# First attention: who empties the head accumulators, and where their two parts are summed

## What is computed

```python
q_r = jnp.einsum('bshq,hqr->bhsr', q_big, W_qr)
k_r = jnp.einsum('bld,hdr->bhlr', kv_r, W_kr)
scores = jnp.einsum('bhsr,bhlr->bhsl', q_r, k_r)
attn = jax.nn.softmax(scores, axis=-1)
ctx_c = jnp.einsum('bhsl,bld->bhsd', attn, kv_r)
ctx_lat = jnp.einsum('bhsd,hkd->bhsk', ctx_c, w_kc_kv)
...
return ctx @ Wo.T
```

## Time and profile before

| | us |
|---|---|
| median of three executions | 1758.19 (1757.7 to 1759.88) |
| the profiled execution, its own time | 1745.59 |
| its span in the trace | 1743.8 |
| TensorE matmul busy | 1652.9 (95%) |
| VectorE busy | 1367.3 (78%) |
| ScalarE busy | 980.1 (56%) |
| GpSimd busy | 924.9 (53%) |

### The profile page before, as it was taken

How to read it: one execution, slowest core, us unless ns; L and a number is a source line. 1 busy time by engine, 2 the same in 40 slices (tenths; PEclk the granted TensorE clock), 3 DMA queues, 4 the chain that set the end, 5 groups by cost and what they waited for, 6 DMA issues and landing times. The chain is left out here.

```text
span 1743.8 us, 48870 instructions
## 1 busy us (share of the span) xinstructions
PE 1652.9 (95%) x16173; PEld 1309.8 (75%) x16173; DVE 1367.3 (78%) x3288; ACT 980.1 (56%) x1903; POOL 924.9 (53%) x620
## 2 busy tenths in 40 slices
PE   5889999999999999999999999999997799997998
PEld 4678888888888888888888888887875445556876
DVE  6888888888988898988889888987874278884223
ACT  5776666666666666666666666665331266662211
POOL 5347777777777777777777777775002022211321
PEclk8699999999999999999999999999998999997999
DMA  9721121121121121122112116113810000005244
GB/s 255 242 67 38 51 72 44 48 74 42 42 81 41 42 70 53 43 61 62 45 48 74 42 47 144 46 50 110 183 25 23 16 13 16 15 7 176 95 150 142
DMA packets 166253, 126.16 MB, mean 72 GB/s; under 512 B 73914, under 2 KB 153448, under 8 KB 165824
## 3 DMA queue, kind: packets, MB, share of 16 engines
q1 hardware_dynamic: 164672, 121.60, 24.7%
q0 software_dynamic: 1536, 3.99, 0.6%
HBM read 82.11 MB, written 24.41 MB: 61 GB/s over the span
## 5 line engine op out<-in xcount | busy, mean ns | idle before, releaser
L1178 POOL TENSOR_TENSOR c_rest<-c_prob 128x1024 f16<-128x1024 f32 (+1 forms) x513 | 799.4, 1575 | 329.6 <-ACT c_prob L962 309.9
L962 ACT ACTIVATE c_prob<-c_psS,ln,c_exp_scale 128x1024 f32<-128x1024 f32 (+1 forms) x514 | 536.9, 1045 | 258.1 <-PE c_psS L797 253.0
L1062 DVE TENSOR_REDUCE c_mxp<-c_psM 128x1 f32<-128x400 f32 (+1 forms) x1040 | 587.0, 571 | 95.0 <-PE c_psM L781 84.5
L797 PE MATMUL c_psS<-c_q,c_kk 128*128 128x256 f16 (+1 forms) x3350 | 512.7, 272 | 0.2 <-issue 0.2
L816 PE MATMUL c_psV<-c_vb,c_prob 128*128 128x129 f16 (+1 forms) x3328 | 396.6, 222 | 0.0
L797 PEld LDWEIGHTS c_psS<-c_q,c_kk 128*128 128x128 f16 (+1 forms) x3350 | 321.9, 99 | 85.7 <-issue 0.4
L819 PE MATMUL c_psV<-c_vb,c_rest 128*128 128x65 f16 (+1 forms) x3328 | 374.1, 193 | 0.0
L781 PE MATMUL c_psM<-c_kkm,c_q 128*128 128x400 f16 (+1 forms) x1040 | 346.1, 333 | 4.6 <-DVE c_mxp L1062 3.0
L816 PEld LDWEIGHTS c_psV<-c_vb,c_prob 128*128 128x128 bf16 (+1 forms) x3328 | 303.8, 97 | 20.5
L819 PEld LDWEIGHTS c_psV<-c_vb,c_rest 128*128 128x128 f16 (+1 forms) x3328 | 301.4, 99 | 21.4
L743 PE MATMUL c_psQ<-c_xb,c_w2s 128*128 128x256 f16 x1188 | 171.2, 276 | 10.5 <-PEq L163 4.1
(11 more groups left out here) (292 smaller groups left out, 2167.6 us busy)
## 6 DMA issues: line engine op xcount, KB each, us to landing
c_w2s<-w_scr SPq DMA_DIRECT2D x66, 256.0 KB, 2.6
c_ms<-m_scr SPq DMA_DIRECT2D x67, 192.0 KB, 2.3
c_w2s<-w_scr SPq DMA_DIRECT2D x66, 128.0 KB, 2.0
acc_scr<-c_acc SPq DMA_DIRECT2D x128, 64.0 KB, 1.6
kv<-acc_scr SPq DMA_DIRECT2D x16, 512.0 KB, 6.5
m_w<-in_L_ffn_W SPq DMA_DIRECT2D x16, 352.0 KB, 4.1
c_vb<-V SPq DMA_DIRECT2D x27, 129.0 KB, 2.0
c_kk<-KK SPq DMA_DIRECT2D x27, 128.0 KB, 2.0
```

The lines of the kernel that those rows point to most:

```text
L797: mm = pe.matmul(psS[g % 2][0:r, i * S:(i + 1) * S], src[:, (lo + i) * P:(lo + i) * P + r], mov[slot][:, :], start=(one == 0 and i % 2 == ...
L962: nc.scalar.activation(prob[g][0:r, 0:w], psS[g % 2][0:r, 0:w], ACT.Exp, bias=keep["ln1024"][0:r, :], scale=exp_scale[slot][0:r, :]).then_ ...
L1062: nc.vector.tensor_reduce(mxp[:, st, c:c + 1], psM[:, st, 0:CHUNKS[c][1]], AX.X, ALU.max).then_inc(mx_done, 1)
L1178: nc.gpsimd.tensor_tensor(rest[g][0:r, 0:w], prob[g][0:r, 0:w], high[0:r, 0:w], ALU.subtract).then_inc(rest_done, 1)
```

## The change

The VectorE drain is taken apart.

- ScalarE copies all 258 columns of `c_psV` into `c_acc`, which grows to 128 x 2 x 129 (two buffers as before). The copy stands at the end of each head's turn, behind `exp(n+1, 1)` and, at odd u, ahead of the `q_other` that opens the next head. It signals `pv_drained`, now once per head.
- GpSimd adds the low to the high sums in place and copies the two denominators into `rec` (`total`), for head n-1 in the turn of head n, between `rest_of(n, 3)` and `rest_of(n+1, 0)`. In turn 0 it does so on a buffer of zeros; `total(N)` follows the loop. So head n has row n+1 of `acc_scr` and of `rec`.
- SyncE's store waits for `total` and takes 64 of each 129 columns.
- The reciprocals are made in two instructions instead of 128: VectorE inverts the 32 denominators of the first batch behind the loop, and the other 224 at the head of the next block.

```diff
         queue.dma_start(keep["acc"][b % 2][:, s],
-                        t["acc_scr"][b * H0:(b + 1) * H0, :, s, :].rearrange("h p d -> p h d")
+                        t["acc_scr"][b * H0 + 1:(b + 1) * H0 + 1, :, s, :].rearrange("h p d -> p h d")
                         ).then_inc(keep["in_acc"][b % 2], 16)
...
     compute.tensor_tensor(rows, rows,
-                          keep["rec"][:, b * H0:(b + 1) * H0, s:s + 1].broadcast_to([P, H0, DC]),
+                          keep["rec"][:, b * H0 + 1:(b + 1) * H0 + 1, s:s + 1].broadcast_to([P, H0, DC]),
                           ALU.mult).then_inc(keep["cs_ready"], 1)
...
     W = 2 * DC + 1
-    acc = [sb(f"c_acc{i}", [P, ST, DC]) for i in range(2)]
+    acc = [sb(f"c_acc{i}", [P, ST, W]) for i in range(2)]
     psS = [ctx.enter_context(nc.psum_tensor(f"c_psS{i}", [P, 1024], F32)) for i in range(2)]
...
     zeroed, filled = sem("c_zeroed"), sem("kk2_filled")
+    acc_zeroed, summed, inverted = sem("acc_zeroed"), sem("summed"), sem("inverted")
     v_ones, v_high, v_low = sem("v_ones"), sem("v_high"), sem("v_low")
...
             sp.sem_inc(sent[0], 16)
-            sp.sem_inc(sent[1], 16)
 
...
                     refill_values(sp, last, 2)
-                sp.wait_ge(pv_drained, 2 * n + 2)
-                sp.dma_start(t["acc_scr"][n], acc[u % 2][:]).then_inc(sent[u % 2], 16)
+                sp.wait_ge(summed, 2 * n + 2)
+                sp.dma_start(t["acc_scr"][n], acc[(u + 1) % 2][:, :, DC:2 * DC]).then_inc(sent[(u + 1) % 2], 16)
                 if last is not None and u == 1:
...
                 if last is not None and u == 3:
+                    sp.wait_ge(pv_done, 4 * n + 8)
                     refill_values(sp, last, 3)
...
             for u in range(2):
-                sp.wait_ge(sent[u], 16 + 16 * (H0 // 2))
+                sp.wait_ge(sent[u], 16 + 16 * H0)
             sp.dma_start(keep["wvo"], keep["wvo_made"][:]).then_inc(keep["in_wvo"], 16)
...
             batch_steps(B - 1, 0)
+            sp.wait_ge(summed, 2 * N + 2)
+            sp.dma_start(t["acc_scr"][N], acc[1][:, :, DC:2 * DC]).then_inc(sent[1], 16)
             for u in range(2):
...
                 if g == 0:
-                    if not isinstance(n, int) or n > 0:
-                        pe.wait_ge(pv_drained, 2 * n)
+                    pe.wait_ge(pv_drained, n + 1)
                 if t0 == 0:
...
             act.sem_inc(exp_done, 2)
+            act.sem_inc(pv_drained, 1)
             for b in range(4):
...
                     exp(n + 1, 1, (u + 1) % AHEAD)
+                    act.wait_ge(pv_done, 4 * n + 8)
+                    act.wait_ge(sent[u % 2], 16 * (2 * j + u // 2) + 16)
+                    nc.scalar.activation(acc[u % 2][:].rearrange("p s w -> p (s w)"), psV[:, 0:ST * W],
+                                         ACT.Copy).then_inc(pv_drained, 1)
 
...
                                                op1=ALU.subtract).then_inc(v_low, 1)
-
-            def drain(n, u, j):
-                dve.wait_ge(pv_done, 4 * n + 8)
-                dve.wait_ge(sent[u % 2], 16 * (2 * j + u // 2) + 16)
-                both = psV[:, 0:ST * W].rearrange("p (s w) -> p s w", s=ST)
-                nc.vector.tensor_reduce(acc[u % 2][:],
-                                        both[:, :, 0:2 * DC].rearrange("p s (t d) -> p s d t", t=2),
-                                        AX.X, ALU.add).then_inc(pv_drained, 1)
-                nc.vector.reciprocal(keep["rec"][:, bass.ds(n, 1), :].rearrange("p o s -> p (o s)"),
-                                     both[:, :, 2 * DC]).then_inc(pv_drained, 1)
 
...
             v_rest(7)
-            dve.wait_ge(v_low, B)
             scale_of(0, 0)
...
                         q_low(p, u - 1)
-                        drain(n, u, j)
                     reduce_max(n + 2, 6)
-                    if u % 2 == 0:
-                        drain(n, u, j)
                     scale_of(n + 2, (u + 2) % AHEAD)
                     reduce_max(n + 2, 7)
+            dve.wait_ge(summed, 2 * H0 + 2)
+            first = keep["rec"][:, 1:H0 + 1, :]
+            nc.vector.reciprocal(first, first).then_inc(inverted, 1)
+            dve.wait_ge(inverted, 1)
             dve.wait_ge(keep["in_acc"][0], 32)
...
 
+            def total(n, i):
+
+                pool.wait_ge(pv_drained, n + 1)
+                nc.gpsimd.tensor_tensor(acc[i][:, :, DC:2 * DC], acc[i][:, :, DC:2 * DC], acc[i][:, :, 0:DC],
+                                        ALU.add).then_inc(summed, 1)
+                nc.gpsimd.tensor_copy(keep["rec"][:, bass.ds(n, 1), :].rearrange("p o s -> p (o s)"),
+                                      acc[i][:, :, 2 * DC]).then_inc(summed, 1)
+
             nc.gpsimd.memset(kk2[0:2 * SHIFT_ROWS, :], SHIFT_ONE).then_inc(filled, 1)
...
                 nc.gpsimd.memset(V[:, b, :, 2 * DC:2 * DC + 1], 1.0).then_inc(v_ones, 1)
+            nc.gpsimd.memset(acc[1][:], 0.0).then_inc(acc_zeroed, 1)
             rest_of(0, 0)
+            pool.wait_ge(acc_zeroed, 1)
+            pool.wait_ge(v_low, B)
             with pool.Fori(0, N // AHEAD) as j:
...
                     rest_of(n, 3)
+                    total(n, (u + 1) % 2)
                     rest_of(n + 1, 0)
+            total(N, 1)
 
...
     in_c, in_x, in_w = sem("in_c"), sem("in_x"), sem("in_w")
-    ones_made, eps_made = sem("ones_made"), sem("eps_made")
+    ones_made, eps_made, inverted = sem("ones_made"), sem("eps_made"), sem("inverted")
     t_full, t_done, o_full, o_done = sem("t_full"), sem("t_done"), sem("o_full"), sem("o_done")
...
             nc.vector.memset(spare[:], 0.0).then_inc(eps_made, 1)
+            later = keep["rec"][:, H0 + 1:B * H0 + 1, :]
+            nc.vector.reciprocal(later, later).then_inc(inverted, 1)
             dve.wait_ge(ones_made, 2)
+            dve.wait_ge(inverted, 1)
             dve.wait_ge(in_c, 80)
...
     "m_scr": (NP0, P, PQ),
-    "acc_scr": (B * H0, P, ST, DC),
+    "acc_scr": (B * H0 + 1, P, ST, DC),
     "xd_scr": (E1 * CAP1, RW),
...
         ident = kv[:, 2 * n_acc + n_wvo:2 * n_acc + n_wvo + P]
-        first = B * LT * DC - B * H0 * ST
-        rec = kv[:, first:first + B * H0 * ST].rearrange("p (n s) -> p n s", s=ST)
+        n_rec = (B * H0 + 1) * ST
+        rec = kv[:, B * LT * DC - n_rec:B * LT * DC].rearrange("p (n s) -> p n s", s=ST)
         layer0 = whole.enter_context(ExitStack())
```

## The result

The changed kernel took 1740.86 us in the median of four executions (1739.63 to 1741.71), the kernel before beside it 1757.95 (1755.78 to 1759.88, four too): a ratio of 0.9903, interval 0.9885 to 0.992, so 17.1 us less. Forecast were 1741.0 us.

What follows compares the result with a forecast made beforehand. TensorE's matmuls were taken to bound the loop over heads, with two recurring waits per pair to win. Terms 6.4 + 10.6 + 0.2 = 17.2 us off 1758.2 gave 1741.0 us, range 1734 to 1758.

Steps and rivals of the forecast that it cites:

- VectorE without the drain: Even heads, maxima pieces 6 to 7: piece 7 starts 0.12 us earlier, removing a 0.10 us stall for `c_mcol`; 6.4 us.
- The release of the accumulator: End of odd heads: ScalarE's copy frees the accumulator 0.18 us earlier, shortening the idle time ahead of `q_first`; 10.6 us.
- the gap at u = 0 closed wholly: Range's lower end: all idle time ahead of `q_first` at u = 0 goes, 2.9 us more than the sum.
- What stands behind the copy: Even u: mirrored copies come 0.39 us later, `maxima(n+2, 0)` still just in time; nothing lost, but no room.
- GpSimd: Per head: one sum and one small copy, taken as 0.6 us, fit in idle time of 1.96 and 1.36 us; no price.
- The 0.25 us of slack in the odd head's chain: Odd heads: GpSimd's second of four groups ends at 703.80, TensorE takes it at 704.05; 0.10 us earlier still fits.
- Stores, reciprocals, ends: Stores cost nothing, landing bounded by 6.2 us; fewer reciprocals and the loop's end win 0.2 us at most.
- VectorE's busy time in the loop: Sign to look for in the loop: VectorE's busy time down by about 73 us, ScalarE's up by 50.
- The pair of 16.95 us: Sign to look for: a pair of heads in the loop takes 16.95 us, from about 17.2 before.

Runs made afterwards that it cites:

- the doubled copy: Changed kernel with ScalarE's accumulator copy made twice in odd heads, first into a spare tile: 1752.1 us, ratio 0.9946 to before; loop 12.9 us longer.
- the kernel that was to do so: Changed kernel with four idle 128 x 128 sums per head on GpSimd ahead of the real one: 1781.45 us, ratio 1.0144 to the kernel before.
- one idle sum: Changed kernel with one more 128 x 128 sum per head on GpSimd, result unread: 1742.0 us against 1760.79 for the kernel before, ratio 0.9891.
- The comparison on another occasion: Changed kernel run again, unchanged, beside the kernel before: 1728.87 us against 1746.98, ratio 0.9893.
- the doubled copy in even heads: Changed kernel with ScalarE's accumulator copy made twice in even heads, first into a spare tile: 1740.97 us, ratio 0.9888 to the kernel before.

## Why the prediction was right

**VectorE without the drain**, 6.4 us: right in mechanism and size. The wait for `c_mcol` is gone, piece 7 comes 0.12 us earlier, and the effect alone is 6.7 us. In odd heads it is nothing, as said.

**The release of the accumulator**, 10.6 us: right in mechanism, its size too small. What failed is "it starts where the mirrored copies start today ... and ends at 710.72". The copy lasted 0.38 us (0.39 predicted), but starts 1.10 us behind the exp's start, where the mirrored copies started 1.23 behind it. So the release is 0.3 us earlier in place of 0.18, and at u = 0 the idle time of 0.27 us falls to nothing and not to 0.09. By the prediction's own working the term is then 32 x 0.15 + 32 x 0.27 = 13.4 us; the doubled copy took 12.9 away. That this end was open was in the range ("the gap at u = 0 closed wholly"), not in the sum. Shown is that the load of `q_first` follows the drain by 0.48 and 0.60 us when nothing else holds it, and that the sequencer's four instructions run in that time. That they alone make it so long is still a reading: no kernel took them away.

**What stands behind the copy**: right. The mirrored copies do not hold `q_first`, and `maxima(n+2, 0)` loads in time, 0.30 us behind their end where the prediction's figures leave 0.22 (711.79 - 711.57) and 0.14 is enough.

**GpSimd**: 0.45 + 0.18 us (0.6 predicted), at no price; one more sum per head would cost nothing either. The 0.25 us of slack in the odd head's chain was never tested at its own scale, since the kernel that was to do so ran into GpSimd's total instead.

**Stores, reciprocals, ends**: 20.45 us in the loop and 20.5 at the end of the block leave 0.0 to 0.1 for the ends (0.2 predicted). The landing of the store has a median of 2.0 us (1.6 before) and at most 2.8, well below the 6.2 that it was bounded by. But the "Nothing" of this term was wrong at one place. From the timeline of the changed kernel, SyncE and ScalarE:

```profile
1055.24 9.38 SPq L512 DMA_DIRECT2D kv<-acc_scr  x4
...
1068.08 0.62 SPq L697 DMA_DIRECT2D acc_scr<-c_acc  x1
...
1070.99 0.39 ACT L1018 ACTIVATE c_acc<-c_psV 128x258 f32<-128x258 f32 x1 [1.15 <-DMA acc_scr<-c_acc]
```

Before the last batch SyncE issues the loads of the head results, and a store stands behind them. Its sum was made at 1057.83, but it is issued at 1068.08 only, so ScalarE's copy waits 1.2 us for the buffer and TensorE 1.0 us for the copy. In the kernel before the store is late there too (1087.41), and nobody waits for it. In every profile of the changed kernel and of its variants with one idle sum or none ScalarE waits there, for 0.9 to 1.2 us. Landing time alone was priced, not the time that a store stands behind other issues.

VectorE's busy time in the loop fell by 45 us and not by 73: the two groups that left made 73.6 us, but instructions that follow each other closely overlap in the records (the drain of the earlier trace rows started at 701.56, 0.09 us before piece 6 ended), so a union of busy time counts them short. Likewise ScalarE's rose by 34 us and not by 50. The pair of 16.95 us came from dividing 1095.60 us by 64 pairs, but between the fourth and the last exp lie 382 of them, six to a pair, so 63.7 pairs: a pair took 17.2 us and takes 16.9.

**The sum and the total.** Against its own profile the kernel should have run in 1728.4 us and ran in 1741.71; carried over to the medians, 1741.0 were predicted and 1740.86 measured. That the median fits so well is partly luck: the loop gave 3.2 us more than the sum, mostly by the release, and would have given about 1 us more still without the late store, and the part behind the block took between 530 and 547 us in the profiles of this study. The comparison on another occasion gave 18.1 us, two variants with the loop of the changed kernel (the doubled copy in even heads and one idle sum) 19.8 and 18.8, the marks in the trace 20.4, and the interval of the first ratio reaches from 14.1 to 20.2. All of them are in the predicted range.

## To carry to other kernels

Put marks into a trace (the same instruction near both ends of the loop) and compare the distance between them: here it repeats to some tenths of a microsecond or better, where the rest of the program moved by 17 us. Before a change frees a resource earlier, look for the least distance between release and use in both kernels; it says what the release is worth, and when an earlier one stops paying. And before adding work to an engine with idle time, compare its total per turn with the turn of the engine that bounds, not only the idle time at the place where it goes.

## What was not expected of the hardware

ScalarE starts its next instruction before the record of the last one ends: 0.10 us before the end of an exp of 1024 columns (698.31 and 698.41), 0.11 us in two copies in a row (706.38 and 706.49), and an idle instruction of 0.19 us delayed what followed by 0.10. Durations of a timeline added up give too late an end. Not every follower does so: the mirrored copies started 0.03 us behind the end of the exp in the kernel before (710.33 and 710.30) and 0.02 behind that of the copy in the changed one, and why they don't overlap the runs do not say. It was this start that I had taken for the copy's.

On GpSimd four sums that each wait for a semaphore of the one before took 0.51 us each in the mean (2.05 us for four); in the kernel with one idle sum, the real one, which does not wait for it, started 0.42 us behind it (711.50 and 711.92).
